# Soft-expert stages: logits by slot from a transposed copy instead of a second product

## The reference, cut to what matters

```
xn     = layernorm(x, gamma, beta)
logits = einsum('bnd,des->bnes', l2norm(xn) * scale, l2norm(mu))   # 512 tokens x 256 slots per batch row
dispatch = softmax(logits, axis=tokens)                            # per slot, over the 512 tokens
combine  = softmax(logits, axis=slots)                             # per token, over the 256 slots
slot_in  = dispatch^T . xn ; slot_out = expert MLP(slot_in) ; out = combine . slot_out
x = x + 0.5 * out
```

## Time and profile before

| | |
|---|---|
| median of 3 runs | 1045.39 us (1043.42 to 1049.7) |
| the profiled execution's own time | 1045.39 us |
| its span, first to last instruction | 1043.6 us |
| busy: PE, PEld, DVE, ACT, POOL | 789.7, 520.1, 675.5, 511.3, 429.7 us |
| mean granted TensorE clock | 0.861 of full speed |
| steps of the first mix stage | about 432 to 495 us of the span |
| steps of the second mix stage | about 947 to 1011 us of the span |

### The profile page before, as it was taken

One profiled execution on the slowest core, in us unless ns is written; L12 is line 12 of the kernel. 1 busy time (PEld: TensorE's weight loads), 2 busy tenths in 40 slices (PEclk: granted clock), 3 DMA queues, 4 the chain that ended last, 5 costly groups with the idle time before them and its releaser, 6 DMA issues.

```text
span 1043.6 us, 18846 instructions
## 1 busy us (share of the span) xinstructions
PE 789.7 (76%) x5628; PEld 520.1 (50%) x5628; DVE 675.5 (65%) x2458; ACT 511.3 (49%) x1374; POOL 429.7 (41%) x495
## 2 busy tenths in 40 slices
PE   4689882987598840798834888988989898828977
PEld 3578772646497830576711322433433333316757
DVE  4555555685755549465662787888888897564644
ACT  5323331524143315665310366757667677667660
POOL 1047772300277735110632476475475533261100
PEclk9999996895599975799965588989989899969998
DMA  5821123002011140000013442232222300000002
GB/s 148 246 62 49 49 48 89 1 18 63 18 51 50 48 99 0 1 2 1 2 20 49 55 62 32 34 57 31 42 46 31 50 4 3 3 0 1 1 1 82
DMA packets 53427, 42.97 MB, mean 41 GB/s; under 512 B 9861, under 2 KB 48722, under 8 KB 53328
## 3 DMA queue, kind: packets, MB, share of 16 engines
q1 hardware_dynamic: 45920, 30.96, 14.7%
q0 software_dynamic: 4992, 9.32, 3.4%
q10 hardware_dynamic: 2416, 1.48, 0.7%
HBM read 18.27 MB, written 11.40 MB: 28 GB/s over the span
## 4 chain that ended last, share of the span: by engine, by line
PE 44%; DVE 17%; issue 13%; ACT 10%; POOL 8%; DMA 5%; ACTq 1%; SPq 1%; DVEq 0%; POOLq 0%
PE psum L1417 6%; POOL arena L821 5%; PE psum L1402 4%; PE psum L1357 3%; ACT arena L1566 3%; PE psum L1195 3%; PE psum L738 3%; PE psum L1158 3%; PE psum L1167 2%; PE psum L1389 2%; DVE cst L1475 2%; DVE half_stats L439 2%; PE psum L776 2%; POOL result_rows L829 2%; PE psum L1256 2%
## 5 line engine op out<-in xcount | busy, mean ns | idle before, releaser
L1475 DVE CUSTOM_DVE_ANT_0 cst<-psum,rot 128x512 bf16<-128x512 f32 (+3 forms) x512 | 222.8, 486 | 69.1 <-PE psum L1389 63.8
L1566 ACT ACTIVATE arena<-psum 128x512 f32<-128x512 f32 (+1 forms) x384 | 177.9, 533 | 59.4 <-PE psum L1402 52.9
L1389 PE MATMUL psum<-arena 48*128 48x512 bf16 (+3 forms) x512 | 123.2, 334 | 38.4 <-DMA arena<-cut 22.6
L821 POOL DMA_INDIRECT arena<-xhat_rows,gather_row x78 | 76.8, 984 | 154.5 <-DVE scatter_row L638 131.3
L1402 PE MATMUL psum<-arena 51*128 51x512 bf16 (+3 forms) x512 | 113.8, 318 | 11.3 <-ACT arena L1566 7.9
L1653 POOL TENSOR_SCALAR_AFFINE_SELECT arena<-arena 128x384 f32<-128x384 f32 x128 | 63.9, 524 | 128.0 <-ACT arena L1566 127.8
L1417 PE MATMUL psum<-arena 128*32 128x512 f32 (+3 forms) x1024 | 100.3, 491 | 1.9 <-POOL arena L1656 1.9
L829 POOL DMA_INDIRECT result_rows<-arena,scatter_row x78 | 78.6, 1007 | 31.6 <-issue 21.4
L788 PE MATMUL psum<-arena 128*128 x624 | 90.8, 290 | 0.1
L776 PE MATMUL psum<-arena 128*128 128x128 f32 x624 | 87.3, 285 | 1.3 <-DVE arena L650 1.2
L788 PEld LDWEIGHTS psum<-arena 128*128 128x128 f32 x624 | 78.0, 196 | 6.3 <-issue 0.3
(11 more groups left out here) (249 smaller groups left out, 1697.9 us busy)
## 6 DMA issues: line engine op xcount, KB each, us to landing
arena<-cut SPq DMA_DIRECT2D x180, 64.0 KB
xhat_rows<-xh SPq DMA_DIRECT2D x16, 256.0 KB, 2.3
arena<-result_rows SPq DMA_DIRECT2D x8, 512.0 KB, 6.1
x<-in_L_attn_x SPq DMA_DIRECT2D x4, 512.0 KB, 7.7
arena<-in_L_ffn_w SPq DMA_DIRECT2D x1, 2048.0 KB, 9.6
out<-x SPq DMA_DIRECT2D x4, 512.0 KB, 3.2
arena<-xhat_rows,gather_row POOLq DMA_INDIRECT x78, 2.6
result_rows<-arena,scatter_row POOLq DMA_INDIRECT x78, 2.3
```

Source lines behind the costliest of these rows:

```text
L821: pool.indirect_dma_start(xg[:, j % AHEAD, :], None, xhat_dram, bass.IndirectOffsetOnAxis(gather_row[:, j:j + 1], 0)).then_inc(gathered[j ...
L1389: mm = pe.matmul(to[:, col:col + (k + 1) * P], q_stack[b % STACKS][rows, h, k * P:k * P + P], k_stack[b % STACKS][rows, h, 0:(k + 1) * P], ...
L1475: last = nc.vector.tensor_tensor_reduce(masked_scores[:, number % 2, col:col + n_keys], frm[:, col:col + n_keys], mask[:, S - n_keys:], 1. ...
L1566: nc.scalar.activation(prob_e[g % 2][:, j, first:last], bank[MAX_BANKS + number % EXP_BANKS][:, 0:last - first], ACT.Exp, scale=DH ** -0.5 ...
```

## The change

The product `logits_d` is removed. `max_c` now also copies each of its two banks into a tile `logits` in SBUF, behind the reduction of that bank, and counts the copies in a new semaphore `logit_kept`. `exp_c` waits for the copy where it waited for the maximum. `logits_d` becomes eight transposes of 128 x 128 pieces of that tile into the same banks 4 and 5; its first four wait for the copies, two by two. `logits_c` gets a wait for the copies of the block before, and `max_c`, from the third block on, one for the transposes of the block two before it, since `logits` has two buffers.

```diff
+        logits = carve(arena4, 1024, (2, TB, SLOTS))
...
                 def max_c(b):
                     for j in range(2):
+                        if b >= 2:
+                            dve.wait_ge(s["logit_d"], at["logit_d"] + 2 * b - 2)
                         dve.wait_ge(s["logit_c"], at["logit_c"] + 2 * b + j + 1)
                         nc.vector.tensor_reduce(neg_c[:, bass.ds(b, 1), 2 * j:2 * j + 2], bank[2 + j][:].rearrange("p (k s) -> p k s", k=2),
                                                 AX.X, ALU.max, negate=True).then_inc(s["max_c"], 1)
+                        nc.vector.tensor_copy(logits[:, b % 2, 2 * j:2 * j + 2, :].rearrange("p k s -> p (k s)"), bank[2 + j][:]).then_inc(s["logit_kept"], 1)
...
                 def exp_c(b, h):
                     for k in range(TB):
                         t = bass.ds(TB * b + k, 1)
-                        act.wait_ge(s["max_c"], at["max_c"] + 2 * b + k // 2 + 1)
+                        act.wait_ge(s["logit_kept"], at["logit_kept"] + 2 * b + k // 2 + 1)
...
                 def logits_c(b, h):
...
                         pe.wait_ge(s["exp_c"], at["exp_c"] + TB * b)
+                        pe.wait_ge(s["logit_kept"], at["logit_kept"] + 2 * b)
...
                 def logits_d(b, h):
                     if later(b):
                         pe.wait_ge(s["exp_d"], at["exp_d"] + 2 * b)
                     for j in range(2):
-                        pe.matmul(bank[4 + j][:], mu[:, j * P:j * P + P], xT[:, h, :], start=True, stop=True).then_inc(s["logit_d"], 1)
+                        for k in range(TB):
+                            if j == 0 and k % 2 == 0:
+                                pe.wait_ge(s["logit_kept"], at["logit_kept"] + 2 * b + k // 2 + 1)
+                            last = pe.transpose(bank[4 + j][:, k * P:k * P + P], logits[:, h, k, j * P:j * P + P], ident)
+                        last.then_inc(s["logit_d"], 1)
```

More of the change, by code:

```diff
@@ L920, in build @@
         MIX_COUNTS = dict(v=0, centered=GROUPS * BY_ACT, centered_v=GROUPS * (GT - BY_ACT), scaled=B, xn=B, squared=T, norm_sqrt=2, unit_ready=2, unit=B, turned=T,
-                          xT_ready=B, logit_c=2 * B, logit_d=2 * B, max_c=2 * B, max_d=2 * B, exp_c=T, exp_d=2 * B,
+                          xT_ready=B, logit_c=2 * B, logit_d=2 * B, logit_kept=2 * B, max_c=2 * B, max_d=2 * B, exp_c=T, exp_d=2 * B,
                           turn_c0=B, turn_c1=B, turn_d0=B, turn_d1=B, kept_c0=B, kept_c1=B, kept_d0=B, kept_d1=B,
```

## The result

The changed kernel took 1056.76 us (median of five runs, 1055.72 to 1057.5) against 1046.66 (1043.42 to 1049.7): ratio 1.0096, interval 1.0071 to 1.0121, so slower by 10.1 us. Run a second time, with 17 runs of the kernel before beside it, it took 1058.0 against 1044.21: 1.0139, interval 1.0118 to 1.0159. The forecast was 1063, the range 1055 to 1076.

A forecast was written before the change was run, and what follows sets the result against it. Two chains, PE's own work and logits_c-DVE-ACT, reach `slots_in` within 0.3 us; the change delays ACT's. Steps 12.5, heads 2.3 and clock 2.6 us sum to 17.4 on 1045.4: 1063 us, range 1055 to 1076.

The forecast's parts named there:

- What ends a step: Mix-stage step: ACT's `keep_d` copy, queued behind the delayed exponentials, ends 0.89 us late and holds up `slots_in`.
- Two of the signs: Expected in the profile: weight loads of `slots_in` idle over 1 us until ACT; PEclk at 0.5 through the heads.
- The size of a step: Mix-stage step: 0.89 us longer, 9.05 us instead of 8.16; 14 steps give 12.5 us.
- The distances of 0.60: DVE in a step: reductions and copies start 0.60 us apart, so the first copy delays the exponentials by 0.60.
- the wait for the second copy: ACT in a step: the third exponential waits until the second copy ends, 0.29 us of the 0.89.
- the added wait of `max_c`: DVE in a step: wait on an earlier block's transposes, already met a step before, costs nothing.
- PE's saving turns into waiting: PE in a step: its work falls by 0.85 us, but it stands idle until ACT's copy ends.
- The heads and the clock: Start of both mix stages: `exp_d(0)` 1.17 us late in each, 2.3 us; slower TensorE clock there, 2.6 us together.
- the clock term: Heads: without L1167 PE works at 1.2 GHz; 2.2 us in the first stage, 0.4 in the second, together 2.6.
- The clock falls inside the steps: Rival, chance 0.22: clock drops among the steps, 1.95 us each; 1076 if every second step, 1090 if every step.
- The sum: Whole kernel: 12.5 us steps, 2.3 heads and 2.6 clock, 17.4 us added to 1045.4, giving 1062.8.
- the low end: Range's lower limit, 1055: copies at 0.52 us, L1097 0.55 late, clock cost left out, sum 9.5 us.

The follow-up runs named there:

- the new order: Changed kernel with ACT, DVE and PE queues rearranged, transposes split around `slots_in`: 1042.21 us, 0.9975; kernel before in the same order, with products: 1042.72 us, 0.9982.
- the short tail: The kernel with the head by product, plus `turn_c(7)` ahead of `turn_slots(6)` on PE and `max_d(7)`, `keep_c(7)` moved up: 1032.97 us, 0.9903.
- the kernel with the head by product: The new order with transposes, but block 0 by product without copies, and ACT's `keep_c` ahead of `keep_slots`: 1035.67 us, 0.9916.

## Why the prediction was right, point by point

- **What ends a step: right.** ACT's `keep_d`, late behind the exponentials, ends PE's wait (L1204 starts 0.05 us after L1101 ends). Moving that one copy took 11.5 of the 15.7 us out of the mix stages and the whole loss out of the time; leaving the copies and undoing the transposes took nothing away. Both are shown. Two of the signs that I had named did not come: the weight loads of `slots_in` idled 0.89 us and not over 1, and the clock was not at 0.5 through the heads.
- **The size of a step: 0.95 for 0.89.** L1101 starts 4.57 us after `logits_c`, 3.61 before. The distances of 0.60 and the wait for the second copy came as forecast. The 0.07 more is the added wait of `max_c` that I had put at nothing; taking it out gave just that back. Over 14 steps: 13.3 us for 12.5.
- **PE's saving turns into waiting: right**, 0.69 and 0.65 us idle in a step. It shortens the step once ACT's copy no longer queues behind the exponentials: in the new order a step takes 8.13 us with products and 7.70 with transposes, 0.43 less, and with `keep_c` ahead of `keep_slots` 7.57.
- **The heads and the clock: mis-sized.** I had 2.3 us for the heads and 2.6 for the clock, 4.9; the stages leave 15.7 - 13.3 = 2.4 for both. The failed step is the clock term: "I take `turn_tokens`, the transposes, `turn_c` and `logits_c(1)` of that head at 1.2 GHz". It rested on the clock not rising without L1167. It rose at 424 to 425, behind `logits_c(0)` alone, while PE stood idle, and fell at 428; so it was low through most of the transposes, but it rose again before `logits_c(1)` began, which took 1.99 us, as before. In the second stage it rose in the course of `logits_c(1)`, which gained 3.68 - 2.69 = 1.0 us. From the first `turn_tokens` to `logits_c(1)` the heads took 1.6 and 1.9 us longer (11.83 to 13.44, 11.86 to 13.76), 3.5 together; less the 1.0 that is the 2.4 to within 0.1. By stage, 3.4 (1.17 + 2.2) and 1.6 (1.17 + 0.4) were forecast, and it was 1.6 and 0.9.
- **The clock falls inside the steps: refuted.** It was 1.00 through the steps of both stages with PE busy 8.4 of 10 us, and in those of the new order and of the short tail. The Trainium skill, page "TensorE: Matmul & The Clock Gate", Part 4 on PE-mode transpose, says that the full clock doesn't engage for transposes. The first head speaks against it: the clock rose between 431.0 and 431.5, when PE had run nothing but transposes since 426.98. The end of the second stage with the short tail, where the clock fell, agrees with it, and so does the second head, where the clock had fallen before 947, with PE idle, and stayed at 0.50 through the transposes from 947 to 950. So the measurement has both, and what decides between them stays open here.
- **The sum.** 17.4 us forecast, 15.7 and 16.1 in the mix stages, 10.1 and 13.8 in the times. The last difference is in the stretches that the diff does not touch (893.1 us in the profile of before, 887.8 and 888.9 in those of the change). Why these scatter was not tried. That 1056.76 lies inside the range, 1.8 us above its low end, is in part luck: the low end stood for a cheaper copy and no cost of the clock, but the copies cost what I had taken, and what brought the time down is for 5.3 us the rest, which the forecast had left as it was.

## What to carry to other kernels

Before taking work off the busiest engine, look at what its next instruction waits for: here two chains ended within 0.3 us of each other, and the change shortened the one and lengthened the other. When an operation is put in front of something on an in-order engine, walk down that engine's queue: the copy whose lateness cost 13 us belonged to another block and did not need the new data at all, and moving it up one place cost one line. A rearranged algorithm wants its own order: in a new one, and with the product kept for the first block, the transposes made the kernel 1% faster than before, of which the order alone, with products, gave 0.2%.

## What I had not expected of the hardware

- A second wait, on a semaphore that had long been reached, cost DVE 0.07 us at the start of an instruction (idle 0.24 us against 0.17, step 9.11 against 9.04).
- The granted clock rose to 2.4 GHz in a stretch in which PE ran transposes alone, back to back (0.50 at 430 to 431, 1.00 from 431.5), and fell in another in which they ran with pauses (1.00 at 993 to 995, 0.50 from 996), but not in a third (1.00 at 998 to 1002 in the kernel with the head by product). The price of a fall, 1.4 us for one `slots_in`, was more than the 0.6 us that an edit gained in the other stage.
